# Attention softmax denominators: their first half issued ahead of the last two scores of a quarter, and their PSUM bank reserved for longer in the bank plan

## The reference, cut to what matters

```python
x = x + xattn(layernorm(x), ctx, ctx)   # per batch and kv head:
                                        #   weights = softmax(q @ k.T / sqrt(32)) ; out = weights @ v
x = x + ffn(layernorm(x), ...)          # a gate per token picks one of 8 small adapters
```

## Time and profile before

| what | value |
|---|---|
| time, median of 3 runs | 1004.49 us (1004.46 to 1005.07) |
| the profiled execution's own time | 1002.18 us |
| its span, first to last instruction | 1000.4 us |
| mean granted TensorE clock | 0.998 |
| busy: PE, DVE, POOL, ACT | 93%, 90%, 80%, 72% |

### The profile page before, as it was taken

One profiled execution on the slowest core, in us unless ns is written; L12 is line 12 of the kernel. 1 busy time (PEld: TensorE's weight loads), 2 busy tenths in 40 slices (PEclk: granted clock), 3 DMA queues, 4 the chain that ended last, 5 costly groups with the idle time before them and its releaser, 6 DMA issues.

```text
span 1000.4 us, 24586 instructions
## 1 busy us (share of the span) xinstructions
PE 933.3 (93%) x9518; PEld 375.5 (38%) x9518; DVE 901.6 (90%) x1106; ACT 721.8 (72%) x1301; POOL 799.6 (80%) x454
## 2 busy tenths in 40 slices
PE   4789999999999999999999999999999899999996
PEld 3223333333333333333333333333222226777773
DVE  6989999999999999999999999988888876889976
ACT  5388888888888888888888888887777776554540
POOL 7269999999999999999999999999999998222110
PEclk9999999999999999999999999999999999999999
DMA  7876676868686868585858586857556653866324
GB/s 252 214 176 160 137 183 142 190 139 193 131 193 132 189 134 199 125 199 126 199 128 200 130 196 131 191 106 170 114 128 150 154 112 115 265 213 229 147 106 168
DMA packets 319875, 164.18 MB, mean 164 GB/s; under 512 B 182216, under 2 KB 307240, under 8 KB 319760
## 3 DMA queue, kind: packets, MB, share of 16 engines
q1 hardware_dynamic: 319456, 161.76, 65.8%
q0 software_dynamic: 304, 0.85, 0.4%
HBM read 107.58 MB, written 54.53 MB: 162 GB/s over the span
## 4 chain that ended last, share of the span: by engine, by line
PE 65%; DVE 21%; issue 11%; ACT 1%; POOL 1%; DMA 0%; SPq 0%; DVEq 0%; ACTq 0%; POOLq 0%
PE psum L588 18%; PE psum L602 15%; DVE row_max L923 11%; PE psum L550 8%; PE psum L615 6%; PE psum L733 5%; PE psum L576 4%; PE psum L711 4%; PE psum L625 2%; DVE den_t L935 2%; DVE probs L1134 2%; PE psum L699 2%; PE psum L633 1%; DVE row_max L914 1%; DVE o_t L929 1%
## 5 line engine op out<-in xcount | busy, mean ns | idle before, releaser
L862 ACT ACTIVATE probs<-psum 128x512 f32<-128x512 f32 x1024 | 553.0, 596 | 136.2 <-PE psum L588 121.1
L923 DVE TENSOR_REDUCE row_max<-psum 128x4 f32<-128x2048 f32 x248 | 565.2, 2279 | 49.8 <-PE psum L550 49.4
L588 PE MATMUL psum<-q_stack,k_stack 97*32 97x512 f16 x4096 | 332.8, 385 | 5.4 <-ACT probs L862 2.0
L363 POOL TENSOR_TENSOR sums<-probs 128x2048 f32<-128x2048 f32 x63 | 287.9, 4570 | 13.4 <-ACT probs L862 13.3
L351 POOL TENSOR_TENSOR sums<-probs 128x2048 f32<-128x2048 f32 x63 | 287.0, 4555 | 9.3 <-ACT probs L862 9.3
L602 PE MATMUL psum<-probs,v_in 128*32 128x512 f32 x2048 | 267.3, 596 | 3.9
L588 PEld LDWEIGHTS psum<-q_stack,k_stack 97*32 97x32 f16 x4096 | 96.7, 94 | 252.3 <-ACT probs L862 164.8
L550 PE MATMUL psum<-high_mem 32*128 32x512 f16 x992 | 98.0, 384 | 24.7 <-DVE row_max L923 21.1
L602 PEld LDWEIGHTS psum<-probs,v_in 128*32 128x32 f32 x2048 | 58.3, 109 | 83.4 <-issue 54.2
L328 POOL TENSOR_TENSOR o_all<-o_all,o_t 128x512 f32<-128x512 f32 x64 | 81.6, 1275 | 9.2
L323 POOL TENSOR_TENSOR o_t<-o_t,inv 128x512 f32<-128x512 f32 x64 | 67.4, 1053 | 25.1 <-DVE inv L941 25.1
(11 more groups left out here) (119 smaller groups left out, 765.5 us busy)
## 6 DMA issues: line engine op xcount, KB each, us to landing
q_stack<-q_split SPq DMA_DIRECT2D x192, 128.0 KB, 3.4
xa<-in_x_dram SPq DMA_DIRECT2D x32, 512.0 KB, 3.7
o_all<-in_x_dram SPq DMA_DIRECT2D x256, 64.0 KB, 2.4
x_attended<-o_all SPq DMA_DIRECT2D x64, 256.0 KB, 4.6
out_dram<-probs SPq DMA_DIRECT2D x32, 512.0 KB, 2.9
q_split<-prod_mem SPq DMA_DIRECT2D x15, 1024.0 KB, 5.6
xa<-x_attended SPq DMA_DIRECT2D x16, 512.0 KB, 4.5
probs<-x_attended SPq DMA_DIRECT2D x16, 512.0 KB, 4.8
```

The source lines that it names most:

```text
L363: pool.tensor_tensor(sums[:, 2 * u % SUMS], probs[:, u % 2, 0], probs[:, u % 2, 1], ALU.add).then_inc(front_done, 1)
L588: last = pe.matmul(st_ps[row:row + D, bank_of["score", u, n], :], k_stack[:, u % SLOTS, t * P + row:t * P + row + D], q_stack[:, u % SLOTS ...
L862: act.activation(probs[:, s, keys, g, :], st_ps[:, bank_of["score", u, n], :], ACT.Exp, scale=EXP_SCALE).then_inc(exped, 1)
L923: dve.reduce_max(row_max[:, u % 2, t:G * ST:ST], s_ps[:], AX.X).then_inc(reduced, 1)
```

## The change

In the quarters that have `first_denominators`, it is issued after `gather` and ahead of the quarter's rest of scores, not behind them. In the list of the bank plan the denominator stands at the same place, and KEPT for a denominator is 9 places for an even unit and 7 for an odd one instead of 5.

```diff
@@ -206,10 +206,12 @@
                         filled.append(("max", u + 1, 0))
                     if u % 2 == 1 and t < PIECES and whole(tile_of(u)):
                         filled.append(("part", tile_of(u), t))
-                    filled += scores
+                    half = MIDST[u % 2][t] - BEGIN[u % 2][t]
+                    filled += scores[:half]
                     if t == (ST - 1 if u % 2 == 1 else 2) and live(u - 1):
                         filled.append(("den", u - 1, 0))
-            KEPT = {"score": 2, "max": 2, "den": (5, 5), "part": 6}
+                    filled += scores[half:]
+            KEPT = {"score": 2, "max": 2, "den": (9, 7), "part": 6}
             bank_of, bank_before, free_at, last_in = {}, {}, [0] * BANKS, [None] * BANKS
@@ -682,10 +684,10 @@
                                 gather(u - 1, ST - 1)
                         elif live(u):
                             gather(u, t - 1)
+                        if t == (ST - 1 if u % 2 == 1 else 2) and live(u - 1) and live(u):
+                            first_denominators(u - 1)
                         if 0 <= u < UNITS - 1:
                             score_keys(u, MIDST[u % 2][t], BEGIN[u % 2][t + 1])
-                        if t == (ST - 1 if u % 2 == 1 else 2) and live(u - 1) and live(u):
-                            first_denominators(u - 1)
                         if u == UNITS - 1 and t == ST - 1:
                             last_denominators(u - 1)
```

## The result

The changed kernel takes 1036.44 us (median of 4 runs, 1034.16 to 1037.86) against 1004.48: 1.0317 times as long, 95% interval 1.0302 to 1.0332, so **32 us slower**. The forecast was 1033.0 in a range of 1011 to 1042. The profiled executions stand 31.98 us apart (1034.16 against 1002.18) and their spans 32.0 (1032.4 against 1000.4), so the traces hold the whole difference. In the changed kernel's trace the lines of the code are two higher: L590 for the scores, L604 gather, L617 and L627 the halves of the denominators, L552 the plain scores, L864 the exponential, L925 the reduction.

The account below looks back on a forecast made before the run. No engine alone bounds it; late L550s that DVE waits for lengthen each pair of units. Waits of 0.45 and 0.47 us, 0.92 times 31 pairs, add 28.5 to 1002.18 (1030.7), plus 2.3 to the median: 1033.0 us, range 1011 to 1042.

Parts of the forecast that it names:

- The two waits: Delays at Site A and Site B from scores issued 0.86 us later: 0.45 and 0.47 us, 0.92 per pair of units.
- Site A: Even unit's quarter 2, 31 moved halves: score 14 0.49 us late, next L550 late, DVE loses 0.45 us.
- the pair: Two successive attention units, the repeating period: 24.75 us with tiles turned, forecast 25.65 to 25.7; 24.00 without, forecast 24.9.
- Site B: Odd unit's quarter 3, 31 moved halves: next unit's score 1 0.50 us late, costing the pair 0.47 us.
- the part's wait for den_t: Site A: the tile's part 0 takes the denominator's bank and waits for its transpose; 0.2 to 0.3 us without the other delay.
- 31 times: Multiplier over all pairs of units, with or without tiles: 0.92 us for each of 31 pairs, 28.5 us.
- Rival 1: Only one wait is paid: slack after Site B absorbs its delay, Site A costs 31 x 0.45; 1018.5 us; chance 0.15.
- Rival 2: All delay is absorbed, DVE's idle times being slack that the queue order hides; 1004.5 us; chance 0.06.
- rival 4: Each site costs the whole 0.86 us because in-order ACT never catches up; 1057.5 us; chance 0.04.
- Rival 3: Faster: at both sites the half fills a real PE stall ahead of the scores, L550 comes earlier; 984 us; chance 0.08.
- Rival 5: PE's clock drops to 1.2 GHz from more and longer gaps; 1052 us with one such pair, more with each; chance 0.02.

Follow-up runs that it names:

- site B alone: From the changed kernel, first half moved ahead of the two scores in odd units only, bank plan kept: 1018.21 us against 1004.42 for the kernel before.
- the two single sites: Two runs from the changed kernel, first half moved in even units only, 1021.36 us, or odd units only, 1018.21 us, against 1004.42 before.
- half the columns: As the changed kernel, but only columns 0 to 255 of the first half go ahead of the two scores: 1009.34 us against 1004.68 for the kernel before.

## Why the prediction was right

**The two waits.** Each was worked out as a delay of 0.86, less what the chain of score, exponential and next score had to spare. Site A: forecast 0.49 for score 14 and 0.45 for DVE; measured 0.50 at the second L552 and 0.47 at the reduction behind it (6.01 us from the gather, before 5.54), and 0.50 in the pair. Site B: forecast 0.50 for score 1 and 0.47 for the pair; measured 0.49 in the run with site B alone. The pair was forecast 0.92 longer and is 0.98. For 31 pairs that is 1.9 us of the 3.4 by which the result lies above the forecast. The waits were right, but the path from site A to the pair was not quite: the forecast let the loss run through DVE, whose work was to be continuous from there. In the changed kernel the chain that ended last has no DVE row between 414.34 and 440.07 and 14% of exponentials, where the pair before (400.49 to 425.24) has 13% of DVE; PE's own rows carry the 0.50 from score 14 to the next wait. That DVE's 0.45 and PE's 0.50 lie so near each other is why the number did not suffer.

**The bank plan.** The wrong step is "So each score waits for the same exponential as before". By the list two sentences above it, score 15 at site B takes the bank of score 13 where it was that of 12, and score 14 that of 12 where it was 11. I costed the plan at nothing; alone it measures 3.3 us. In the changed kernel exponential 13 has ended 0.8 us before the later score 15 comes, so in its pairs nothing of this is paid. Of the part's wait for den_t I had said 0.2 to 0.3 us without the other delay; it measures 0.38 there, and costs nothing.

**The end and the start.** "31 times" was short at the end. The pairs end with unit 60; from its last gather to that of unit 63 the changed kernel takes 35.55 us against 33.65, 1.90 more. The last site B gives 0.55. The last site A gives the whole 0.86, because unit 62 has no L550 behind it and the scores run straight on. And score 14 of unit 63 waits for exponential 12 by the plan, 0.49, though no half was moved in that unit's order on PE. I had looked at moved halves only. Against 31 equal pairs the last site A's 0.36 and this 0.49 make 0.9 us of the 3.4. Another 0.6 stand ahead of the first unit's gather. There all nine other traces are 0.4 to 1.7 us later than the kernel before's, whatever their edit, so I can't put those 0.6 down to the change.

**The rivals.** Rival 1 (one of the two waits) is refuted by the two single sites and by their sum. Rival 2 (all absorbed) and rival 4 (0.86 each) fall with the pair; half the columns shows why neither could be: the first 0.37 us are absorbed and the rest is paid whole. Rival 3 (a real stall to fill) falls with L552 at 2.25 us from the gather in place of 2.26: no time was gained, so the waits of the loads lay under the running gather. Rival 5: the granted clock is 1.00 over the steady stage (69 to 818 us) in this and in all other traces, with more and longer gaps than before. The Trainium skill, page "TensorE: Matmul & The Clock Gate", section "A second HAM failure mode: psum-queue depth-cycling", tells of a kernel in which short idling between groups of matmuls, while it cycles through PSUM banks, makes the clock fall and rise; the steady stage of none of the ten traces here shows that. The one fall in these traces between the first units and the adapters, at 61.40 us of the half of the columns, came behind 1.84 us of idle time. It also supports a price that rival 5 took from the earlier trace rows alone: there the 603 ns stand at 25.8 to 46.7 us, for which the profile gives a granted clock of 1.00, whereas in this fall four such matmuls together take 0.61 us instead of 0.39.

**What was to be seen.** The pair of 25.65 to 25.7 came out 25.73, 24.9 came out 24.98. ACT's idle time ahead of exponential 11 was forecast 1.1 and is 1.34; exponentials 9 and 10 end 0.19 us earlier against the gather than before, which the forecast had not counted. DVE's wait for L550 was forecast 78 us in all and is 72.3. The time of the pair came out of other rows, so neither of those two moved the sum.

## What to carry to other kernels

Before two pieces of work on an in-order engine are exchanged, look at who takes up each one's result and which buffer its taker must free: work with no urgent reader (an accumulation that is completed later) belongs behind work that feeds the next engine, even where both take the same time and nothing waits in between. The price of a delay is the delay less the slack of that loop, so measure the slack in the trace (here 0.37 us against 0.86). And when a list plans the buffers, compare for every use whose contents it overwrites, to the last unit, including those where nothing else has changed.

## What the runs showed that I had not expected

Matmuls of 32 output columns that write different 32-partition quarters of a bank run side by side: two heads' first half took 0.86 us as four heads' did, and leaving out two heads from the front shortened nothing. Cutting the columns from 512 to 256 did halve it (0.43 us). That doubled the number of the first halves' matmuls and loads (1024 for 512) and showed no cost of its own: the whole came to 4.7 us where 5 was expected without it.
